# Attention stage of a two-layer ViT tower: the stage written out without engine loops, its small steps reordered, and the head sums carried to the output projection by DMA

## What is computed

```
h  = x @ W + pe;  n = layernorm(h)
Q, K, V = (n @ Wq.T + bq), (n @ Wk.T + bk), (n @ Wv.T + bv)    reshaped to (B*8, 1024, 16)
context = softmax(Q K^T / 4) V;   out = context @ Wo.T + bo + n
h = h + layernorm(out) * gamma + beta
```

## Time and profile before

| what | value |
|---|---|
| median of 3 executions | 1697.8 us |
| the profiled execution's own time | 1701.07 us |
| its span | 1699.0 us |
| mean granted TensorE clock over the span | 0.857 |
| busy PE / DVE / ACT / POOL | 1307.3 / 1031.0 / 1014.7 / 522.0 us |
| attention exponentials (L351) | 512, busy 491.6 us |
| idle of ACT ahead of them | 200.7 us |

### The profile page before, as it was taken

How to read it: one execution, slowest core, us unless ns; L and a number is a source line. 1 busy time by engine, 2 the same in 40 slices (tenths; PEclk the granted TensorE clock), 3 DMA queues, 4 the chain that set the end, 5 groups by cost and what they waited for, 6 DMA issues and landing times. The chain is left out here.

```text
span 1699.0 us, 32574 instructions
## 1 busy us (share of the span) xinstructions
PE 1307.3 (77%) x9689; PEld 856.1 (50%) x9689; DVE 1031.0 (61%) x2830; ACT 1014.7 (60%) x1358; POOL 522.0 (31%) x451
## 2 busy tenths in 40 slices
PE   3498998989898999459999857677752299999950
PEld 2244444444443444247777646555652177767740
DVE  6155755555655663427878656666453288888854
ACT  0287887776776889308888733333220188888840
POOL 1212232211222221200000011555444346666665
PEclk8598999998999999769999967766665599999985
DMA  3451516060606150011111000100000445555429
GB/s 78 86 99 33 115 29 113 24 110 6 125 19 114 29 100 2 8 29 48 36 43 45 7 5 3 34 32 30 32 26 27 138 128 141 138 140 145 139 58 296
DMA packets 134491, 119.27 MB, mean 70 GB/s; under 512 B 30460, under 2 KB 112311, under 8 KB 134351
## 3 DMA queue, kind: packets, MB, share of 16 engines
q1 hardware_dynamic: 116814, 96.37, 25.3%
q0 software_dynamic: 9216, 16.94, 2.9%
q10 hardware_dynamic: 8320, 4.19, 0.8%
HBM read 76.63 MB, written 42.37 MB: 70 GB/s over the span
## 5 line engine op out<-in xcount | busy, mean ns | idle before, releaser
L351 ACT ACTIVATE a_probs<-a_psS 128x1024 f32<-128x1024 f32 x512 | 491.6, 1034 | 200.7 <-PE a_psS L429 186.9
L441 PE MATMUL a_psO<-a_probs,a_v 128*32 128x256 f32 x4096 | 284.9, 397 | 8.3 <-DVE a_o_sb L640 7.7
L803 ACT ACTIVATE f_g_hi<-f_psH,f_b_hid 128x512 fp32r<-128x512 f32 x288 | 201.4, 699 | 68.0 <-PE f_psH L71 44.7
L429 PE MATMUL a_psS<-a_qs,a_ks 50*128 50x512 f32 x1024 | 195.9, 462 | 59.2 <-issue 28.4
L918 DVE TENSOR_TENSOR f_g_lo<-f_g,f_g_hi 128x512 fp32r<-128x512 f32 x288 | 197.6, 688 | 68.8 <-ACT f_g L805 64.0
L1734 POOL DMA_INDIRECT result<-f_out,f_idx x160 | 188.2, 1176 | 131.2 <-DVEq L1758 74.4
L805 ACT ACTIVATE f_g<-f_psH,f_b_hid 128x512 f32<-128x512 f32 x288 | 201.1, 698 | 0.0
L441 PEld LDWEIGHTS a_psO<-a_probs,a_v 128*32 128x32 f32 x4096 | 109.1, 111 | 156.0 <-issue 92.7
L1160 POOL DMA_INDIRECT queue<-all_row,all_idx x128 | 126.6, 989 | 104.7 <-DVEq L1550 48.1
L429 PEld LDWEIGHTS a_psS<-a_qs,a_ks 50*128 50x128 f32 x1024 | 80.0, 193 | 133.1 <-issue 75.4
L1245 POOL TENSOR_TENSOR a_rs<-a_veps,all_half 128x8 f32<-128x8 f32 x16 | 26.7, 1668 | 352.7 <-DVE a_veps L83 352.6
(11 more groups left out here) (284 smaller groups left out, 2263.8 us busy)
## 6 DMA issues: line engine op xcount, KB each, us to landing
f_raw<-W SPq DMA_DIRECT2D x80, 256.0 KB
a_qs<-qparts SPq DMA_DIRECT2D x96, 128.0 KB, 4.5
a_ks<-kparts SPq DMA_DIRECT2D x96, 128.0 KB, 4.8
f_rows<-queue SPq DMA_DIRECT2D x40, 260.0 KB
qparts<-a_parts SPq DMA_DIRECT2D x16, 512.0 KB, 2.6
kparts<-a_parts SPq DMA_DIRECT2D x16, 512.0 KB, 3.2
f_raw<-w SPq DMA_DIRECT2D x32, 256.0 KB, 2.6
out_y<-result SPq DMA_DIRECT2D x8, 512.0 KB, 11.7
```

The lines of the kernel that those rows point to most:

```text
L351: nc.scalar.activation(probs[u % NPR][:, :], psS[score_buffer(u)][:, :, :].rearrange("p a n -> p (a n)"), ACT.Exp).then_inc(exp_done, 1)
L429: last = nc.tensor.matmul(psS[score_buffer(u)][:, p, :], ks[par][64 * p:64 * p + KG, kt, hp * P:(hp + 1) * P], queries(par, hp, p, a), sta ...
L441: last = nc.tensor.matmul(psO[32 * g:32 * g + 32, a * HALF:(a + 1) * HALF], v[par][:, 2 * hp + p, kt, :], probs[u % NPR][:, cols:cols + HA ...
L803: nc.scalar.activation(g_hi[i][:, n, :], psH[n][:, :], ACT.Gelu, bias=b_hid[i][:, n:n + 1])
```

## The change

- `rounds` writes out all 8 batches; no engine loops in this stage.
- New places in `STEPS` and `FIRST`: q and k of both chunks come before N and v; `RESCUE` moves from burst 27 to 26, and the wait for `stack_in` moves from `rescue` to the first scores of a batch (and into the branch not taken). `UPPER`, `LOWER` and `APPLY` shift with them.
- `nT`, `nT_hi`, `nT_lo`, `qf` and `sq` get a buffer for each chunk.
- The transposes are gone. Columns 16 to 31 of `v` are all ones, so rows 16 to 31 of each group in `psO` all hold the denominator. SP's queue carries `o_sb` to DRAM by eight DMAs, waits for them, and brings it back as `sums` by one (`spread`). DVE takes the reciprocal of 128x256 denominators and multiplies (burst 5 of the next pair), and PE projects in burst 6. `spread` stands ahead of `redistribute` in SP's program for pairs 0 and 1, ahead of `send_guard` for pair 2, and alone for pair 3.
- For batch 0 alone, q goes round by SP's queue and k by ACT's.
- Set-up: the constant rows of `ks` are filled by POOL, not DVE; PE starts on the token weights without waiting for the position table, and DVE alone waits for that; the branch of the bound is taken ahead of v.
- The end of the stage: `spread`, divide, project in place of turn, divide, turn back, copy, project.

```diff
-    STEPS = {0: ("E", 0), 4: ("E", 1), 5: ("T", 0), 8: ("q", 0), 12: ("k", 0), 13: ("v", 0), 14: ("T", 1), 15: ("N", 0),
-             16: ("q", 1), 20: ("k", 1), 22: ("N", 1), 23: ("v", 1)}
-    TURN, BACK, PROJECT = 1, 2, 3
-    RESCUE = 27
-    UPPER = {3: "add_bias", 7: "normal", 10: "moments", 11: "second", 13: "score"}
-    LOWER = {21: "add_bias", 24: "normal", 27: "moments", 28: "second", 29: "score"}
-    APPLY = {1: 0, 6: 1}
-    PSA_PAIR, PSA_EMBED = 3, len(STEPS)
+    STEPS = {0: ("E", 0), 2: ("E", 1), 5: ("T", 0), 8: ("q", 0), 10: ("k", 0), 12: ("T", 1), 16: ("q", 1), 18: ("k", 1),
+             20: ("N", 0), 23: ("N", 1), 26: ("v", 0), 29: ("v", 1)}
+    FIRST = [("E", 0), ("E", 1), ("T", 0), ("q", 0), ("k", 0), ("T", 1), ("q", 1), ("k", 1), ("N", 0), ("N", 1), ("v", 0), ("v", 1)]
+    DIVIDE, PROJECT = 5, 6
+    RESCUE = 26
+    UPPER = {6: "add_bias", 9: "normal", 14: "moments", 15: "second", 17: "score"}
+    LOWER = {22: "add_bias", 24: "normal", 27: "moments", 28: "second", 30: "score"}
+    APPLY = {1: 0, 7: 1}
+    PSA_PAIR, PSA_EMBED = 1, len(STEPS)
...
-            for par in range(2):
-                batch(par, par, par == 1, True)
-            with eng.Fori(1, B // 2 - 1) as it:
-                for par in range(2):
-                    batch(it * 2 + par, par, True, True)
-            for par in range(2):
-                batch(B - 2 + par, par, True, par == 0)
+            for b in range(B):
+                batch(b, b % 2, b > 0, b + 1 < B)
...
+            def spread(pair):
+
+                sp.wait_ge(o_evac, pair + 2)
+                for p in range(2):
+                    for cc in range(2):
+                        for w in range(2):
+                            row = 64 * p + 32 * cc + DH * w
+                            sp.dma_start(dsum[64 * cc:64 * cc + 64, w, p, :].rearrange("(i d) t -> d i t", d=DH),
+                                         o_sb[row:row + DH, :].rearrange("d (i t) -> d i t", t=P)).then_inc(sums_out, 16)
+                sp.wait_ge(sums_out, (pair + 1) * 8 * 16)
+                if pair:
+                    sp.wait_ge(ctxT_done, pair)
+                sp.dma_start(sums[:, :, :, :], dsum).then_inc(sums_in, 16)
+
             def batch(b, par, prior, more):
...
+                for q in range(HP):
+                    spread(b * HP + q)
+                    if more and q < CPB:
+                        redistribute(sp, b + 1, 1 - par, 0, q)
+                        redistribute(sp, b + 1, 1 - par, 1, q)
+                    if more and q == 2:
+                        send_guard(b + 1, 1 - par)
...
             sp.wait_ge(cleared, 2)
-            redistribute(0, 0)
+            for ch in range(CPB):
+                redistribute(sp, 0, 0, 0, ch)
             send_guard(0, 0)
...
+            act.sem_inc(kparts_out, 16)
+            act.wait_ge(cleared, 2)
+            for ch in range(CPB):
+                redistribute(act, 0, 0, 1, ch)
+            rounds(batch)
...
                 if u == 0:
+                    pe.wait_ge(stack_in, (b + 1) * STACK)
                     pe.wait_ge(guard_in, (b + 1) * GUARD)
...
                     dve.drain()
-                    dve.sem_inc((qf_done, kf_done)[i], 1)
                     dve.wait_ge((qparts_out, kparts_out)[i], n * 16)
-                    nc.vector.tensor_copy(hi, src)
+                    nc.vector.tensor_copy(hi, src).then_inc((qf_done, kf_done)[i], 1)
...
             def out_of_psum(b, hp):
+                if b or hp:
+                    dve.wait_ge(sums_out, (b * HP + hp) * 8 * 16)
...
             def divide(pair):
+                dve.wait_ge(sums_in, (pair + 1) * 16)
+                nc.vector.reciprocal(rden[:, :, :], sums[:, 1, :, :])
+                dve.drain()
+                nc.vector.tensor_tensor(ctxT[:, :, :], sums[:, 0, :, :], rden[:, :, :], ALU.mult).then_inc(ctxT_done, 1)
...
-            dve.wait_ge(tok_in, 16 * N_TOK)
+            dve.wait_ge(pe_in, 16)
```

More of the change, by code:

```diff
@@ L322, in batch, with clear @@
                         finish(LOWER[m], b, 0)
[L324 to L328, removed]
+            def clear(par):
+                nc.gpsimd.memset(v[par][:, :, :, DH:], 1.0)
+                for q in range(2):
+                    pool.drain()
+                    nc.gpsimd.memset(ks[par][64 * q + 32:64 * q + 64, :, :].bitcast(F32), 1.0)
+                pool.drain()
+                pool.sem_inc(cleared, 2)
+            clear(0)
             for kind, ch in FIRST:
@@ L331, in _ @@
             pool.drain()
[L332 to L341, removed]
+            clear(1)
+            rounds(batch)
             for part in UPPER.values():
@@ L443, in weigh @@
                 last.then_inc(pv_done, 1)
-            def turn(pair):
-                pe.wait_ge(o_evac, pair + 2)
-                for i in range(4):
-                    last = nc.tensor.transpose(psA[:, i * P:(i + 1) * P], o_sb[:, i * P:(i + 1) * P], ident[:, :])
-                last.then_inc(ht_ps, 1)
-            def turn_back(pair):
-                pe.wait_ge(ctx_done, pair + 1)
-                for p in range(2):
-                    last = nc.tensor.transpose(psA[:, p * P:(p + 1) * P], ctx_tm[:, p, :, :].rearrange("p j d -> p (j d)"), ident[:, :])
-                last.then_inc(ct_ps, 1)
             def project(pair):
@@ L480, in batch @@
                         embed_step(*STEPS[m], b + 1, 1 - par, psA[:, :])
-                    if r in (TURN, BACK, PROJECT) and (q or prior):
+                    if r == PROJECT and (q or prior):
                         pe.wait_ge(psA_free, uses.next())
-                        {TURN: turn, BACK: turn_back, PROJECT: project}[r](pair)
+                        project(pair)
             pe.sem_inc(pv_done, NPR)
-            pe.wait_ge(tok_in, 16 * N_TOK)
+            pe.wait_ge(tok_in, 16)
             for kind, ch in FIRST:
@@ L494, in _ @@
                 scores(0, 0, u)
-            rounds(pe, batch)
+            pe.wait_ge(psA_free, 1)
+            rounds(batch)
             uses = Tally((B - 1) * PSA_BATCH - PSA_PAIR + PSA_PAIR * HP)
-            for step in (turn, turn_back, project):
-                pe.wait_ge(psA_free, uses.next())
-                step(B * HP - 1)
+            pe.wait_ge(psA_free, uses.next())
+            project(B * HP - 1)
         @block.vector
@@ L627, in guard @@
                 dve.drain()
-                dve.wait_ge(guard_in, b * GUARD) if not (isinstance(b, int) and b == 0) else None
+                if b:
+                    dve.wait_ge(guard_in, b * GUARD)
                 dve.wait_ge(unsafe_done, b + 1)
@@ L704, in _ @@
             for kind, ch in FIRST[2:]:
+                if kind == "v" and ch == 0:
+                    guard(0)
                 embed_read(kind, ch, 0, 0, FIRST_PS[kind, ch], False)
@@ L708, in _ @@
             dve.sem_inc(psA_free, 1)
-            guard(0)
-            rounds(dve, batch)
+            rounds(batch)
             out = B * HP - 1
             divide(out)
-            evacuate(out)
             add_input(out, (B - 1) % 2, HP - 1)
```

120 lines of the change are left out of this document (48 added, 72 removed).

## The result

The changed kernel takes 1728.7 us by the median of four executions, beside 1698.6 for the kernel before on the same chip: a ratio of 1.0164 (95% interval 1.0127 to 1.0202). I had forecast 1685 and a range up to 1708. The profiled execution took 1732.0 us, with a span of 1730.2.

A forecast was written before the change was run, and what follows sets the result against it. PE's program order was taken to bound batches 0 to 6, with SP's queue eating the gain. From 1701.07 us, minus 10.6 (batches), minus 9 (set-up), plus 7 (end) gave 1688.5, 1685 as median; range 1630 to 1708.

The forecast's parts named there:

- T: End of DVE's copy of pair 0 in a batch, from which the chain to the guard is counted.
- Loops: Batches 2 to 5: looped ones take 8.9 us more than written-out ones; writing them out can save 36 us.
- Set-up: Before the first exponential: k on ACT's queue 4 us, position table 2, v and branch 3; 9 us gained.
- End of the stage: After the last copy: spread, landing, divide and projection take 11 us against 3.6, uncovered; 7 us lost.
- Lower clock: Behind PE's 3.5 us wait for the guard, TensorE drops to its lower clock; 3.9 us a batch.
- Reciprocal: DVE's division of 128x256 takes 1.7 us; about 4 us more a batch fits its idle, except 1.2 in burst 5.
- SP's queue: Spreads, chunks and guard in series land the guard at T + 52.2; PE, there at T + 48.65, waits 3.5 us.
- That delay lies before the guard and costs nothing beside it.: Second pair's sums arrive at T + 29, with PE 0.7 to 1.4 us early at its projection; priced at nothing.
- The new order "should take away the other waits": Embedding batches: the new step order removes PE's other waits for `psA`, 2.6 us together in batch 6.
- Rival 2: Guard's landing: SP's queue is slower, guard at T + 55.8, each microsecond costs 7; 1710 us; chance 0.22.
- Rival 1: SP's queue keeps up; batches of 70 to 72 us without guard wait; 1644 us, 1625 at best; chance 0.27.
- Rival 3: The loop is not the cost: idle at `rescue` stays near 5 us written out; 1685 to 1700; chance 0.05.

The follow-up runs named there:

- run 11: Kernel before with loops written out, new set-up and chunk buffers, transposes and old step order kept, second v at burst 23; other chip: 1625.7 us, ratio 0.9703.
- run 1: Kernel before with only the loops written out, all 8 batches: 1670.1 us, ratio 0.9797.
- run 2: Changed kernel with PE's transposes in place of the carriage by DMA, new order and set-up kept: 1672.0 us, ratio 0.9815.
- Run 5: Changed kernel with DVE taking 16 reciprocals a row in place of 256, queue unchanged: 1702.2 us, ratio 1.0037.
- run 9: Changed kernel with two extra waited 64 KB stores ahead of the guard on SP's queue; other chip: 1736.7 us, ratio 1.0355.
- run 3: Changed kernel with the guard's DMAs ahead of the third spread in SP's program: 1728.4 us, ratio 1.0169.
- run 6: Changed kernel with k's write and returns issued by ACT in every batch, not by SP: 1663.0 us, ratio 0.9804.
- run 10: run 6 with DVE's division one burst earlier, parts of the final normalisation moved and one drain added; other chip: 1642.5 us, ratio 0.9806.
- run 7: Kernel before with loops written out, new set-up and chunk buffers, transposes and old order, but second v at burst 24: 1657.8 us, ratio 0.9761.
- run 8: run 7 without PE's flag read and branch in batches 1 to 7: 1656.8 us, ratio 0.9769.

## Why the prediction was wrong, point by point

The five stretches were forecast at 616.9 us and take 649.9: 10.6 us gained became 22.4 lost, a miss of 33.0. Seven times the guard's delay of 4.7 us is 32.9. SP's rows put the delay on the chain from T to the guard in every batch: in the mean of the seven the guard is issued 52.9 us behind T (51.4 to 54.1), where the forecast had 47.2. From the issue to the next T it is 30.8 us in the first six, forecast 31.7, and of that the landing took 4.1 in batch 4 for the forecast's 5.0; so behind the landing nothing is missing. The rest of the miss, 1728.7 against 1685, is mostly 2.3 us of set-up, 0.9 at the end of the stage, and the 6.1 behind the mark, in code that is the same, which is scatter.

The stage as a whole, at the mark, along a path of edits (run 11 on the other chip, so the two rows with it are the least sure; by the ratios the order costs 1.1%, 19 us):

| part | from, to | us |
|---|---|---|
| loops written out | before, run 1 | -23.1 |
| set-up, chunk buffers, place of the wait for q and k | run 1, run 11 | -19.5 |
| new order of small steps | run 11, run 2 | +11.9 |
| sums carried by DMA | run 2, after | +55.7 |
| sum | before, after | +25.0 |

- *Loops.* 36 us forecast, 23.1 at the mark; the ratio gives 34. The mechanism held; which of the two sizes is right is open.
- *Set-up.* 9 forecast, 6.7 measured after, 9.3 in run 11 (first exponential at 60.80). The time went the way of the reading by which DMA engines that are already full gain little from a second queue; the first exponential near 52 us would have been the other. Another 10 of the row above lie in the batches, 6.7 of them in batch 0 (83.7 to 77.0); no run told the chunk buffers apart from scatter between executions there.
- *End of the stage.* 7 forecast, 7.9 measured.
- *Lower clock.* 3.9 us a batch forecast, behind the guard's wait. It came at least once in each of the seven batches, but in two of them, 1 and 4, behind the idle at the branch (3.6 and 2.6 us; granted clock 0.60 from 218.1 to 223.1 and 0.57 from 467.9 to 471.8). I had put no idle above 2.5 us there. In batch 0 it came behind a wait of 2.5 us (0.50 from 143.6 to 147.8), and in batch 4 once more, briefly, behind two waits of 1.4 and 1.6 us (0.72 from 422.3 to 428.4). So the idle of 3.22 us that I went by is not the shortest that brings it. In batches 1 and 4 the term is missing behind the guard, and the reciprocal cost more there than I had put; that the stretch behind the landing comes out as forecast is in part luck.
- *Reciprocal.* 1.7 us forecast, 1.75 measured. Its cost was a smaller step that failed: "about 4 us more a batch, which its idle takes", with 1.2 a batch at one place. Run 5 gets 1.8 a batch back by removing it, most of it between the guard and the next T, where two of the four divisions stand and the chain to the guard does not cover them. That is 0.6 more than the 1.2, and small beside the queue's 4.7.
- *SP's queue.* The step that failed is the size of this term: "the guard lands at T + 52.2", measured T + 56.9. The path was right, its landings were put too short. By the rows of batch 4 the three spreads take 6.1, 7.0 and 6.7, together 19.8 where I had 17.4; q's chunks 7.2 and 6.5, so 13.7 for 11.0; k's 8.8 and 10.5, so 19.3 for 18.0; the guard 4.1 for 5.0. My bound of 8.5 held the spreads; for q's write I gave none above 2.6, which its measured 3.9 asked for. I took the rows of DMAs that ran alone, where nearly each of these is issued right behind others. Behind q's chunk and k's, that the earlier ones were still draining is my reading; the rows show 4.9 us for a lone spread's stores and 6.7 for the same behind k's returns.
- *"That delay lies before the guard and costs nothing beside it."* PE waits some 1.0 to 1.4 us for the sums at three projections of batch 4, and for the copy at each pair's end. Waits at the projections in bursts 14 and 22 were my sign that the sums and not the guard come too late. In this kernel the guard still sets the time (run 9); but with the guard moved ahead (run 3) the sums set the same time, so a second chain of about equal length stood behind the first.
- *The new order "should take away the other waits".* Run 2 shows the reverse: +11.9 us against run 11, with waits for the copy out of PSUM of 23.3 us against 5.3.
- *Rivals.* Rival 2 was right in place, mechanism and price per microsecond (run 9). It had 0.22 and 1710 with the guard at T + 55.8. At T + 56.9 its own price gives 1718, since q and k were late as well, not the spreads alone; the other 11 us to 1729 are mostly the set-up's shortfall and the scatter behind the mark. Rival 1 fell: no embedding batch takes under 80 us. Rival 3 fell with run 1.

## What to carry to other kernels

A queue whose program waits for each landing is a serial engine. Before something is added to it, add up landings as they are behind other transfers, not those of a lone DMA, and see when the last item is due. Here, trading 1.1 us of transposes a pair for a round trip through DRAM did not pay even with another engine issuing part of it: runs 6 and 10 are at 0.980 and 0.981 of the kernel before, run 11 with its transposes at 0.970.
Where DVE's copy out of the accumulator is late, PE stands still; moving one small step next to it, from burst 23 to 24, cost 14.1 us at the mark, 0.6% by the ratio (runs 7 and 11).

## What the runs showed that I had not expected

- The same bytes by a second issuer saved 46.6 us at the mark, where the set-up, with k on ACT's queue as one of its edits, gained 6.7 in all.
- PE idles at a branch over a long block in written-out code as well, 17.1 us in seven (run 1), but taking the branch out brings 5 us at the mark and none in the ratio (run 8).
- The stages behind the attention, the same code in all kernels, took between 948.7 and 987.8 us in single executions. Two of the runs on the other chip have the shortest, 948.7 and 950.1, and the third 962.6 against 966.8 and more elsewhere, so the marks there may be closer to comparable than the times. One execution of this kernel can't settle a question of 1%; the mark of a stage can do better, within its own scatter.
